# Four stacked graph networks on one core: five of 25 gathered columns picked by TensorE in the relation passes, twelve in the convolutions

## The chip, the core and the metric

The kernel runs on one core of a Trainium2 chip. Its time is the device time of one execution in microseconds (us), the median of three runs. A core has TensorE (PE, matrix products into PSUM), VectorE (DVE), ScalarE (ACT), GpSimd (POOL, here the issuer of indirect DMAs) and SyncE (SP, here the issuer of plain DMAs). Each engine works through its own instructions in order and waits on semaphores for the others.

## What is computed

Node features `x` (12,500 nodes, 16 channels) go through four graph layers, each followed by a residual sum and a layer norm. There are 400,000 edges, sorted by destination. Cut to what matters:

```python
# layer 0: a weight matrix per edge, from the edge's attributes
h = relu(edge_attr @ W1 + b1); w = (h @ W2 + b2).reshape(-1, 16, 16)
out = segment_sum(einsum('ei,eio->eo', x[src], w), dst) + x @ root
# layer 1: two graph convolutions, each over all edges
msg = (x @ W.T)[row] * norm[:, None];  out = segment_sum(msg, col) + b
# layer 2: relation matrices of 230 types, on a hyperbolic ball
msg = exp_map(einsum('ei,eio->eo', h_tan[src], rel_weight[etype]) + rel_emb[etype])
h_agg = weighted segment means of msg by dst
# layer 3: relation matrices of 90 types, times an attention term e
msg = einsum('ei,eio->eo', h[src], W_rel[rel_type]) * e;  out = segment_sum(msg, dst)
```

All five passes over the edges have one thing in common: each edge needs the row of a small node table at its source node `src`.

## The kernel before

**Passes and chunks.** Pass 0 is layer 0, passes 1 and 2 are the two graph convolutions, pass 3 and pass 4 are the relation layers with 230 and 90 types. The 400,000 edges lie as 128 partitions by 3,125 columns. A pass takes them in 125 chunks of 25 columns (`CH`), in a loop of 25 rounds by five slots (`S`).

**Table rows.** A column is 128 edges, one per partition. Its 128 table rows come in one of two ways. Either POOL issues one indirect DMA for the column (L571). Or TensorE *picks* it: the node's number is taken apart as `q * 100 + m * 25 + r`; ScalarE turns the spread code of the column into four one-hot matrices over `q`, one for each bank `m` (L849 the distance to the partition's number, L855 the one-hot); TensorE multiplies them by the table, split into two parts for accuracy (`tparts`), in 4 x 2 products of 400 columns that add up in one PSUM bank (L726); VectorE multiplies the 16 x 25 candidates by a mask of `r` (`sel`, L1282; product L1287) and adds up over the 25 (L1276). `PK` says how many of the 25 columns of a chunk are picked: before, 11 in passes 1 and 2, none elsewhere. They are handled in groups (`GRP`) of 3, 3, 3 and 2 columns that take turns in two halves of PSUM.

**A relation chunk.** ScalarE makes one-hots of the edge types (L892 distances, L901 one-hots, in two halves of 12 and 13 columns); TensorE selects each edge's matrix with them (L784, seven groups of four columns, four products a column in pass 3 and two in pass 4); VectorE multiplies by the gathered rows (L1129) and reduces (L1124), group by group, one reduction behind; between them stand small steps of the previous chunk in pass 3 (`finish`). A scan under the run mask (L804 on ScalarE, L1100 on VectorE) gives running sums per destination (L1103), which SP stores. `norms` on ScalarE (L883, L885) waits for VectorE's squared norms of the previous chunk (L1410) and stands ahead of the second half of the one-hots.

**Order.** Every engine's order is written out by hand. `chunk_in` on VectorE waits, ahead of everything else of a chunk, for its stored, gathered and loaded semaphores. SP loads a chunk's indices once the chunk five before it is done. After a pass POOL gathers the last running sum of each node (L580), VectorE does the node-wise work, and the next table is stored.

## Time and profile before

| | us |
|---|---|
| median of three runs | 17383.71 |
| lowest and highest | 17378.82, 17388.19 |
| the profiled execution | 17386.87 |
| its span | 17385.1 |

| engine | busy us | share of the span |
|---|---|---|
| PE | 10661.7 | 61% |
| DVE | 11826.2 | 68% |
| ACT | 6431.9 | 37% |
| POOL | 12857.9 | 74% |

By the first L571 of each pass and the first L580 behind it, the passes lie at 86 to 4077, 4241 to 6460, 6633 to about 8854, 9030 to 13031 and 13228 to 17226 us. Busy shares are means over these stages; what a pass is worth must be read from the chunk that repeats in it. A row of the timeline gives start, duration, engine, line, operation, tiles and count, and in brackets how long the engine had been idle and what ended it.

### The profile page before, as it was taken

What the parts mean: (1) busy time and instruction counts of PE and PEld (TensorE: products, weight loads), DVE (VectorE), ACT (ScalarE), POOL (GpSimd) and SP (SyncE); (2) the same over time, 40 slices, a digit from 0 to 9 for tenths busy, and PEclk for the clock granted to TensorE, in tenths of its full rate; (3) what the DMA queues carried; (4) which work ended last, traced back from release to release, by engine and by line L of the source; (5) the groups of instructions that cost most, each with busy time, mean ns of one, the idle gap of its engine ahead of it and who ended that gap; (6) DMA issues with size and microseconds to landing.
All of it is one profiled execution on the core that took longest, in us unless ns stands there. A gap on an engine that the chain in (4) does not pass through costs nothing.

```text
span 17385.1 us, 175951 instructions
## 1 busy us (share of the span) xinstructions
PE 10661.7 (61%) x53964; PEld 9557.6 (55%) x53964; DVE 11826.2 (68%) x12509; ACT 6431.9 (37%) x5440; POOL 12857.9 (74%) x13391
## 2 busy tenths in 40 slices
PE   6777777774999977999945555555552333333332
PEld 4555555554999977999944444544441333333332
DVE  6777777775777765777746666666664666666664
ACT  1111111112666655666634444444441222222221
POOL 6777777776777776777767777777766777777776
PEclk8888888887999998999977777777775555555555
DMA  1111111111222211222211111111111222222221
GB/s 34 27 28 28 27 28 28 27 27 27 41 41 40 40 34 33 40 41 41 39 32 38 41 41 39 40 41 41 38 40 34 46 47 45 47 47 45 46 47 30
DMA packets 811052, 649.12 MB, mean 37 GB/s; under 512 B 434919, under 2 KB 729495, under 8 KB 810245
## 3 DMA queue, kind: packets, MB, share of 16 engines
q0 software_dynamic: 428000, 138.55, 9.4%
q1 hardware_dynamic: 382882, 509.02, 9.3%
q14 instruction: 150, 1.23, 0.0%
q8 instruction: 20, 0.33, 0.0%
HBM read 480.45 MB, written 166.09 MB: 37 GB/s over the span
## 4 chain that ended last, share of the span: by engine, by line
POOL 73%; issue 24%; DVE 1%; DMA 0%; PE 0%; DVEq 0%; SPq 0%; POOLq 0%; ACT 0%; ACTq 0%
POOL deep L571 71%; POOL deep L580 3%; SPq L352 0%; DVE big L1129 0%; DVEq L926 0%; DMA wgt<-in_edge_weight 0%; PE PS L726 0%; DMA wide<-in_edge_attr 0%; DMA deep<-running,endi 0%; DVEq L1134 0%; DMA deep<-table,idx 0%; POOLq L565 0%; DVE deep L1220 0%; PE PS L748 0%; POOLq L568 0%
## 5 line engine op out<-in xcount | busy, mean ns | idle before, releaser
L571 POOL DMA_INDIRECT deep<-table,idx x12875 | 12374.5, 961 | 4205.8 <-issue 3922.1
L726 PE MATMUL PS<-tparts,hot 125*128 125x400 f32 x22000 | 4081.5, 346 | 497.2 <-DVE big L1287 324.9
L726 PEld LDWEIGHTS PS<-tparts,hot 125*128 125x128 f32 x22000 | 3997.6, 188 | 580.9 <-DVE big L1287 407.7
L1129 DVE TENSOR_TENSOR big<-PS,deep 128x768 f32<-128x768 f32 (+4 forms) x2750 | 2986.5, 1086 | 1610.6 <-DMA deep<-table,idx 957.1
L784 PE MATMUL PS<-wx,hot 115*128 115x272 f32 x12500 | 2040.5, 329 | 1939.6 <-ACT hot L901 1513.0
L784 PE MATMUL PS<-w,hot 90*128 90x256 f32 x6250 | 1517.8, 429 | 2647.5 <-DVE big L1129 2445.8
L784 PEld LDWEIGHTS PS<-wx,hot 115*128 115x128 f32 x12500 | 1933.4, 226 | 2046.6 <-issue 1539.6
L784 PEld LDWEIGHTS PS<-w,hot 90*128 90x128 f32 x6250 | 1370.8, 327 | 2794.3 <-DVE big L1129 2603.0
L687 PE MATMUL PS<-w0b_sb,big 128*128 128x256 f32 x6250 | 1909.8, 457 | 1025.5 <-DVE big L1129 989.5
L687 PEld LDWEIGHTS PS<-w0b_sb,big 128*128 128x128 f32 x6250 | 1406.1, 231 | 1594.0 <-DVE big L1129 1122.5
L855 ACT ACTIVATE hot<-deep,ones_col 128x1536 fp32r<-128x1536 bf16 x1000 | 1445.0, 1469 | 1409.1 <-PE PS L726 1369.1
L1124 DVE TENSOR_REDUCE acc<-big 128x64 f32<-128x1024 f32 (+2 forms) x1875 | 1939.8, 1035 | 18.4
L901 ACT ACTIVATE hot<-deep,ones_col 128x3072 fp32r<-128x3072 bf16 (+1 forms) x500 | 1142.0, 2284 | 1855.0 <-PE PS L784 1855.0
L1287 DVE TENSOR_TENSOR big<-PS,shared 128x1200 f32<-128x1200 f32 x1000 | 1303.6, 1304 | 603.4 <-PE PS L726 513.8
L804 ACT ACTIVATE mask<-same 128x425 bf16 x625 | 342.7, 548 | 3277.2 <-DVE msg L1103 3276.6
L849 ACT ACTIVATE deep<-wide,negbank 128x1408 bf16<-128x1408 f16 x1000 | 1387.8, 1458 | 73.6 <-DMA wide<-pick_codes 37.3
L1276 DVE TENSOR_REDUCE deep<-big 128x48 f32<-128x1200 f32 x1000 | 1291.3, 1291 | 18.3
L819 ACT ACTIVATE big<-PS,b0a_sb 128x512 f32<-128x512 f32 x1000 | 581.3, 595 | 1784.5 <-PE PS L670 1784.5
L892 ACT ACTIVATE deep<-wide,negrel 128x3200 bf16<-128x3200 bf16 x375 | 1097.3, 2957 | 58.2 <-DMA wide<-edge_types 21.9
L1124 DVE TENSOR_REDUCE msg<-big 128x64 f32<-128x1088 f32 x875 | 1011.2, 1156 | 17.3
L1473 DVE TENSOR_TENSOR sml<-term,deep 128x25 f32<-128x25 f32 x125 | 27.9, 223 | 1346.1 <-DMA deep<-table,idx 1346.1
L670 PE MATMUL PS<-atT,tabo 128*128 128x512 f32 x2000 | 883.7, 536 | 0.0
(267 smaller groups left out, 6076.6 us busy)
## 6 DMA issues: line engine op xcount, KB each, us to landing
deep<-table,idx POOLq DMA_INDIRECT x12875
wide<-edge_types SPq DMA_DIRECT2D x250, 800.0 KB, 4.3
wide<-pick_codes SPq DMA_DIRECT2D x250, 352.0 KB, 3.5
running<-msg SPq DMA_DIRECT2D x250, 212.5 KB, 2.1
running<-msg SPq DMA_DIRECT2D x250, 200.0 KB, 2.0
running<-msg SPq DMA_DIRECT2D x125, 400.0 KB, 2.5
wide<-in_edge_attr SPq DMA_DIRECT2D x125, 200.0 KB
idx<-in_src SPq DMA_DIRECT2D x625, 12.5 KB
```

The costliest lines, as they stand in the source:

```text
L571: pool.indirect_dma_start(g[:, j, 0:GW[l]], None, tab_dram[l][:, :], bass.IndirectOffsetOnAxis(ap=idx[:, s, j:j + 1], axis=0)).then_inc(ga ...
L687: last = pe.matmul(PS[:, b, (u % 2) * CC:(u % 2) * CC + CC], hsb[:, k % 2, u * P:u * P + P], w0b_sb[:, :], start=True, stop=True)
L726: last = pe.matmul(o, poneh[0:NQ, m, c], tparts[0:NQ, k, m * JC:m * JC + JC], start=m == 0 and k == 0, stop=m == BK - 1 and k == 1)
L784: last = pe.matmul(o, oneh[0:K, h, (t0 + u) * P:(t0 + u) * P + P], rhs, start=z == 0, stop=z == len(parts) - 1)
L849: last = act.activation(pdist[:, m, :], code[:, 0:NPK * P], ACT.Abs, bias=negbank[:, m:m + 1])
L855: act.activation(poneh[:, :, c], pdist[:, :, c], ACT.Relu, bias=ones_col[:, 0:1], scale=-1.0).then_inc(poneh_ready, 1)
L892: last = act.activation(dist[:, h, :], rows_b[:, HOME[s], :], ACT.Abs, bias=negrel[:, h:h + 1])
L901: act.activation(oneh[:, 0:halves, c], dist[:, 0:halves, c], ACT.Relu, bias=ones_col[:, 0:1], scale=-1.0).then_inc(oneh_ready, 1)
L1124: dve.tensor_reduce(m[:, groups[j][0], col:col + C], products(j), AXX, ALU.add)
L1129: dve.tensor_tensor(products(j), matv(l, j, n), xs, ALU.mult).then_inc(mats_free, 1)
L1276: return dve.tensor_reduce(gatv(s, l)[:, CH - n + t0:CH - n + t0 + w, :], chosen[:, i % 2, 0:w], AXX, ALU.add)
L1287: dve.tensor_tensor(chosen[:, i % 2, 0:w], PS[:, b:b + w, 0:JC].rearrange("p t (c r) -> p t c r", r=JR), sel[:, t0:t0 + w].unsqueeze(2).to ...
```

## The change

`PK` becomes 12 in passes 1 and 2, and 5 in passes 3 and 4, so POOL issues 13 and 20 indirect DMAs per chunk there in place of 14 and 25. The fourth convolution group has three columns in place of two. A relation chunk gets two groups of picks (three and two columns, of 400 columns in PSUM in pass 3, 426 in pass 4, whose table rows are 17 wide) ahead of the seven groups of matrices, on the same semaphores `mats` and `mats_free`, with PSUM banks from a table. Their one-hots (`rhot`) and distances (`rdist`) are ScalarE's, from five columns of the same codes, which one more DMA per chunk spreads. `run_mask` goes behind the one-hots. The wait for the gathers leaves `chunk_in` and stands behind the picks (`columns_in`) in all four passes. Tables of passes 3 and 4 are also split (`table_parts`), and SP waits for that ahead of their first spread; at a pass's start all five slots' loads are issued ahead of the first spread. Some buffers have new homes.

```diff
-    PK = [0, 11, 11, 0, 0]
+    PK = [0, 12, 12, 5, 5]
-    GRP = [(0, 3), (3, 3), (6, 3), (9, 2)]
+    GRP = [(0, 3), (3, 3), (6, 3), (9, 3)]
+    RGRP = [[], [], [], [(0, 3), (3, 2)], [(0, 3), (3, 2)]]
+    BANKS = [[(2 * (k % 2), 2) for k in range(8)], None, None, [(0, 3), (4, 2)] + [(4 * (i % 2), 4) for i in range(6)] + [(3, 1)],
+             [(0, 3), (3, 2), (5, 2), (0, 2), (2, 2), (4, 2), (6, 2), (3, 2), (7, 1)]]
...
             def spread_rows(l, it, s):
+                if l >= 3:
+                    c0 = (NPK - RPK) * P
+                    sp.dma_start(rcodes[:, HOME[s], :],
+                                 code_dram[bass.ds(it * S + s, 1), c0:c0 + RPK * P].rearrange("a n -> (a n)").partition_broadcast(P)
+                                 ).then_inc(rows_in[s], 16)
...
                 for s in range(S):
                     load(l, 0, s)
+                if l >= 3:
+                    sp.wait_ge(tab_st, 16 * (l + 1))
+                    sp.wait_ge(ev[f"parts{l}"], 1)
+                for s in range(S):
                     if l and s:
                         spread_rows(l, 0, s - 1)
...
+                        for i, (t0, n) in enumerate(RGRP[l]):
+                            mats_wait(l, c0 + ng * s, it, i)
+                            for u in range(n):
...
+                                for m in range(BK):
+                                    for k in range(2):
+                                        last = pe.matmul(o, rhot[0:NQ, m, c], tparts[0:NQ, k, m * pc:m * pc + pc],
+                                                         start=m == 0 and k == 0, stop=m == BK - 1 and k == 1)
+                            last.then_inc(mats, 1)
...
             def one_hots(l, it, s, first):
+                for m in range(BK):
+                    act.activation(rdist[:, m, :], rcodes[:, HOME[s], :], ACT.Abs, bias=negbank[:, m:m + 1])
                 for h in range(halves):
                     last = act.activation(dist[:, h, :], rows_b[:, HOME[s], :], ACT.Abs, bias=negrel[:, h:h + 1])
                 last.then_inc(rows_used, 1)
                 act.drain()
-                run_mask(l, it, s)
+                act.wait_ge(mats, it * (S * ng) + (o0 + ng * s - ng + NPG[l]))
+                act.activation(rhot[:, :, :], rdist[:, :, :], ACT.Relu, bias=ones_col[:, 0:1], scale=-1.0).then_inc(poneh_ready, 1)
                 for b, (t0, n) in enumerate(HALF):
...
+                run_mask(l, it, s)
                 act.drain()
...
-                dve.wait_ge(gathered[s], it * (16 * (CH - PK[l])) + (ga_base(l) + 16 * (CH - PK[l])))
                 dve.wait_ge(loaded[s], it * (16 * LOADS[l]) + (ld_base(l) + 16 * LOADS[l]))
+
+            def columns_in(l, it, s):
+
+                dve.wait_ge(gathered[s], it * (16 * (CH - PK[l])) + (ga_base(l) + 16 * (CH - PK[l])))
...
                 for j, (tiles, n) in enumerate(groups):
+                    if j == pg:
+                        columns_in(l, it, s)
```

Two places where the order moves. On VectorE in a convolution chunk, from the last picks of a chunk to the first of the next (`picks` is TensorE's signal, `gathered` POOL's), before:

```order
L1287 TENSOR_TENSOR big<-PS,shared 128x800 [waits picks]
L1276 TENSOR_REDUCE deep<-big 128x48
L1276 TENSOR_REDUCE deep<-big 128x32
L1295 TENSOR_TENSOR acc<-deep,wgt 128x25x16
L1096 REGISTER_ALU
L1100 SCALAR_TENSOR_TENSOR acc<-mask,acc 128x416 [waits masked]
L1102 COPY acc<-acc 128x16
L1103 COPY msg<-acc 128x400
L1109 REGISTER_ALU
L1282 ISA [waits loaded2,gathered2,stored0]
L1282 TENSOR_TENSOR shared<-PS,late 128x275
```

and now:

```order
L1362 TENSOR_TENSOR big<-PS,sel 128x1200 [waits picks]
L1353 TENSOR_REDUCE deep<-big 128x48 x2
L1371 TENSOR_TENSOR acc<-deep,wgt 128x25x16 [waits gathered1]
L1148 REGISTER_ALU
L1152 SCALAR_TENSOR_TENSOR acc<-mask,acc 128x416 [waits masked]
L1154 COPY acc<-acc 128x16
L1155 COPY msg<-acc 128x400
L1161 REGISTER_ALU
L1172 ISA [waits loaded2,stored0]
L1172 TENSOR_TENSOR sel<-PS,rsel 128x300
```

The gathers of the next chunk are no longer waited for ahead of its picks, and the last product has 1,200 elements in place of 800. On VectorE at a chunk's start in pass 3 (`mats` is TensorE's signal), before:

```order
L1410 TENSOR_SCALAR sml<-sml 128x25
L1129 TENSOR_TENSOR big<-PS,deep 128x1088 [waits loaded3,mats,gathered3,stored1]
L1129 TENSOR_TENSOR big<-PS,deep 128x1088 [waits mats]
L1124 TENSOR_REDUCE msg<-big 128x4x16
L1129 TENSOR_TENSOR big<-PS,deep 128x1088 [waits mats]
```

and now:

```order
L1488 TENSOR_SCALAR sml<-sml 128x25
L1172 TENSOR_TENSOR sel<-iota_f,rsel 128x125 [waits loaded4,stored4]
L1204 TENSOR_TENSOR big<-PS,sel 128x1200 [waits mats]
L1204 TENSOR_TENSOR big<-PS,sel 128x800 [waits mats]
L1193 TENSOR_REDUCE deep<-big 128x3x16
L1204 TENSOR_TENSOR big<-PS,deep 128x1088 [waits mats,gathered4]
L1193 TENSOR_REDUCE deep<-big 128x2x16
L1204 TENSOR_TENSOR big<-PS,deep 128x1088 [waits mats]
```

A mask, two products and two reductions stand ahead of the first product that needs a gathered column. On ScalarE in pass 4, before:

```order
L892 ACTIVATE deep<-wide,negrel 128x3200 [waits rows_in1]
L803 REGISTER_ALU
L804 ISA [waits chunks_done]
L804 ACTIVATE mask<-same 128x17x25
L899 REGISTER_ALU
L901 ACTIVATE hot<-deep,ones_col 128x1536 [waits mats]
L899 REGISTER_ALU
L901 ACTIVATE hot<-deep,ones_col 128x1664 [waits mats]
```

and now:

```order
L940 ACTIVATE late<-tabo,negbank 128x640 [waits rows_in1]
L940 ACTIVATE late<-tabo,negbank 128x640 x3
L942 ACTIVATE deep<-wide,negrel 128x3200
L945 REGISTER_ALU
L946 ACTIVATE rhot<-late,ones_col 128x2560 [waits mats]
L950 REGISTER_ALU
L952 ACTIVATE hot<-deep,ones_col 128x1536 [waits mats]
L950 REGISTER_ALU
L952 ACTIVATE hot<-deep,ones_col 128x1664 [waits mats]
L847 REGISTER_ALU
L848 ISA [waits chunks_done]
L848 ACTIVATE mask<-same 128x17x25
```

Five activations are new, and the mask with its wait for VectorE's finished chunks stands last.

## Rows read from the trace of the kernel before

**Rows 1.** The page's part 4, the chain that ended last, by engine.

```profile
POOL 73%; issue 24%; DVE 1%; DMA 0%; PE 0%; DVEq 0%; SPq 0%; POOLq 0%; ACT 0%; ACTq 0%
```

**Rows 2.** Instructions of L571 in passes 1, 2, 3, 4: duration ns min/median/max, first and last start.

```profile
L571 POOL DMA_INDIRECT deep<-table,idx x1750: 940/944/1197, 4240.7 to 6438.5; - x195
...
L571 POOL DMA_INDIRECT deep<-table,idx x1750: 940/944/1464, 6633.4 to 8832.2; - x195
...
L571 POOL DMA_INDIRECT deep<-table,idx x3125: 940/944/1932, 9029.7 to 12994.3; - x196
...
L571 POOL DMA_INDIRECT deep<-table,idx x3125: 940/944/1727, 13227.6 to 17199.4; - x196
```

**Rows 3.** Windows inside passes 1, 3, 4: PE, PEld, DVE, ACT, POOL, clock, DMA, GB/s.

```profile
4300.00:6400.00 2100.00, 1944.85 (x10510) 1905.22 (x10509) 1618.72 (x1551) 1404.93 (x1075) 1590.80 (x1672) 1.00 0.21 40
9200.00:12900.00 3700.00, 1901.08 (x11642) 1800.86 (x11641) 2492.85 (x3385) 1760.14 (x1051) 2811.09 (x2918) 0.75 0.18 40
13400.00:17100.00 3700.00, 1414.06 (x5824) 1277.12 (x5824) 2308.31 (x2329) 775.29 (x466) 2813.34 (x2910) 0.50 0.22 46
```

**Rows 4.** Timeline of one chunk of pass 1, TensorE and VectorE.

```profile
5000.72 16.29 PE L726 MATMUL PS<-tparts,hot 125*128 125x400 f32 x88 [1.22 <-DVE big L1287]
...
5008.30 0.99 DVE L1287 TENSOR_TENSOR big<-PS,shared 128x800 f32<-128x800 f32 x1 [0.20 <-PE PS L726]
...
5009.21 2.45 DVE L1276 TENSOR_REDUCE deep<-big 128x48 f32<-128x1200 f32 x2
...
5016.15 0.45 DVE L1282 TENSOR_TENSOR shared<-PS,late 128x275 f32<-128x275 f32 x1 [1.20 <-DMA deep<-table,idx]
...
5018.26 2.08 PE L726 MATMUL PS<-tparts,hot 125*128 125x400 f32 x10 [1.25 <-DVE big L1287]
5018.36 1.41 DVE L1287 TENSOR_TENSOR big<-PS,shared 128x1200 f32<-128x1200 f32 x1 [0.16 <-issue]
```

**Rows 5.** Timeline of VectorE in pass 3: a chunk's first products, and the next chunk's.

```profile
11001.05 1.29 DVE L1129 TENSOR_TENSOR big<-PS,deep 128x1088 f32<-128x1088 f32 x1 [7.74 <-DMA deep<-table,idx]
11002.50 1.29 DVE L1129 TENSOR_TENSOR big<-PS,deep 128x1088 f32<-128x1088 f32 x1 [0.16 <-issue]
...
11033.08 1.29 DVE L1129 TENSOR_TENSOR big<-PS,deep 128x1088 f32<-128x1088 f32 x1 [9.05 <-DMA deep<-table,idx]
```

**Rows 6.** Timeline of ScalarE, then of TensorE, in the same chunk of pass 3.

```profile
11028.34 3.06 ACT L901 ACTIVATE hot<-deep,ones_col 128x3328 fp32r<-128x3328 bf16 x1
...
11034.42 6.37 PE L784 MATMUL PS<-wx,hot 115*128 115x272 f32 x48 [2.79 <-DVE big L1129]
```

**Rows 7.** Timeline of VectorE, then of TensorE, in one chunk of pass 4.

```profile
15008.84 1.23 DVE L1129 TENSOR_TENSOR big<-PS,deep 128x1024 f32<-128x1024 f32 x1 [0.16 <-issue]
15010.23 1.22 DVE L1129 TENSOR_TENSOR big<-PS,deep 128x1024 f32<-128x1024 f32 x1 [0.17 <-issue]
...
15040.06 0.20 DVE L1473 TENSOR_TENSOR sml<-term,deep 128x25 f32<-128x25 f32 x1 [10.34 <-DMA deep<-table,idx]
...
15021.51 5.49 PE L784 MATMUL PS<-w,hot 90*128 90x256 f32 x24 [0.42 <-DVE big L1129]
```

**Rows 8.** Timeline of TensorE in pass 0: two equal groups behind idle times of different length.

```profile
3036.24 2.93 PE L687 MATMUL PS<-w0b_sb,big 128*128 128x256 f32 x6 [4.14 <-DVE big L1129]
...
3067.60 1.56 PE L687 MATMUL PS<-w0b_sb,big 128*128 128x256 f32 x6 [2.71 <-DVE big L1129]
```

**Rows 9.** Timeline at pass ends (POOL) and in the node-wise work between them (VectorE).

```profile
6460.20 0.94 POOL L580 DMA_INDIRECT deep<-running,endi  x1 [20.74 <-DMA running<-msg]
...
9041.51 0.42 DVE L1046 TENSOR_TENSOR w<-big,w 90x256 fp32r<-90x256 f32 x1
...
13031.09 0.94 POOL L580 DMA_INDIRECT deep<-running,endi  x1 [35.83 <-DMA running<-msg]
...
13216.00 1.82 DVE L1467 TENSOR_REDUCE na<-Y 125x100 f32<-125x1600 f32 x1
...
17226.24 1.31 POOL L580 DMA_INDIRECT deep<-running,endi  x1 [25.91 <-DMA running<-msg]
```

More of the change, by code:

```diff
@@ L85, in build_gnn @@
     JC = C * JR
-    GRP = [(0, 3), (3, 3), (6, 3), (9, 2)]
+    PW = [0, C, C, C, C + 1]
+    PCOL = [(w * JR + 1) // 2 * 2 for w in PW]
+    GRP = [(0, 3), (3, 3), (6, 3), (9, 3)]
+    RGRP = [[], [], [], [(0, 3), (3, 2)], [(0, 3), (3, 2)]]
+    NPG = [len(g) for g in RGRP]
     NGR = len(GRP)
@@ L90, in build_gnn @@
     PRIOR = [3, 3, 2, 2, 5]
-    PICKED = [1, 2]
+    PICKED = [1, 2, 3, 4]
+    RPK = PK[3]
+    assert PK[4] == RPK and 3 * (C + 1) * JR <= 1600
     LOADS = [3, 2, 2, 1, 2]
     NAT = (CH + 7) // 8
-    GROUPS = [[(slice(k, CH, 8), len(range(k, CH, 8))) for k in range(8)], None, None] + 2 * [[(slice(t, t + n), n) for t, n in QUADS]]
+    GROUPS = [[(slice(k, CH, 8), len(range(k, CH, 8))) for k in range(8)], None, None] + [
+        [(slice(CH - PK[l] + t, CH - PK[l] + t + n), n) for t, n in RGRP[l]] + [(slice(t, t + n), n) for t, n in QUADS] for l in (3, 4)]
+    BANKS = [[(2 * (k % 2), 2) for k in range(8)], None, None, [(0, 3), (4, 2)] + [(4 * (i % 2), 4) for i in range(6)] + [(3, 1)],
+             [(0, 3), (3, 2), (5, 2), (0, 2), (2, 2), (4, 2), (6, 2), (3, 2), (7, 1)]]
     MATS = [0, 3, 4]
@@ L239, in build_gnn @@
         flat_b = Y[:, :].bitcast(BF16)[:, 0:TILES]
-        VT = shared[:, 0:13 * NQ].rearrange("p (b n) -> p b n", n=NQ)
+        ohr = Y[:, :].bitcast(BF16)[:, 0:CH * NJ].rearrange("p (t r) -> p t r", r=NJ)
+        VT0, VT = (t[:, 0:13 * NQ].rearrange("p (b n) -> p b n", n=NQ) for t in (big2, late))
         tabo = sb("tabo", [P, NJ * 17])
-        rsel = late[:, 0:NCH * NPK]
-        sel = shared[:, 0:NPK * JR].rearrange("p (t r) -> p t r", r=JR)
+        rsel = sb("rsel", [P, NCH * NPK], BF16)
+        sel = sb("sel", [P, NPK, JR])
+        rhot = sb("rhot", [P, BK, RPK * P], F32R)
+        rdist = Z.bitcast(BF16)[:, 0:RPK * BK * P].rearrange("p (m n) -> p m n", m=BK)
+        rcodes = tabo[:, 0:3 * RPK * P // 2].bitcast(F16).rearrange("p (k n) -> p k n", k=3)
         chosen = big2[:, 0:6 * JC].rearrange("p (g t c r) -> p g t c r", g=2, t=3, r=JR)
+        rprod = big2[:, 0:3200].rearrange("p (k n) -> p k n", k=2)
         w0blk = tabo[:, 0:8 * HID].rearrange("p (k h) -> p k h", h=HID)
@@ L592, in transposes, with node_product @@
                 last.then_inc(ready, 1)
-            def node_product(kron, done):
+            def node_product(kron, done, of=VT):
                 for b, (c0, n) in enumerate(BLK):
-                    last = pe.matmul(PSF[0:NQ, c0:c0 + n], VT[0:n, b, :], kron[0:n, 0:n], start=True, stop=True)
+                    last = pe.matmul(PSF[0:NQ, c0:c0 + n], of[0:n, b, :], kron[0:n, 0:n], start=True, stop=True)
                 last.then_inc(done, 1)
@@ L646, in mats_wait @@
             def mats_wait(l, m, it, j):
-                slots, n = SLOTS[l], len(GROUPS[l])
-                back = j - slots + 1 if j >= slots else max(k for k in range(n) if k % slots == j % slots) + 1 - n
-                pe.wait_ge(mats_free, it * (S * n) + (m + NPR + back))
+                n, (b, w) = len(BANKS[l]), BANKS[l][j]
+                ago = next(d for d in range(1, n + 1) if BANKS[l][j - d][0] < b + w and b < sum(BANKS[l][j - d]))
+                pe.wait_ge(mats_free, it * (S * n) + (m + MFREE + j - ago + 1))
             NG0 = len(GROUPS[0])
@@ L831, in flip @@
                     for b in range(0, len(blocks), 4):
-                        c0, n = blocks[b][0], min(4, len(blocks) - b) * P
-                        last = act.copy(to[:, c0:c0 + n], PS[:, 4 + b // 4, 0:n])
+                        c0, n = blocks[b][0], sum(k == P for _, k in blocks[b:b + 4]) * P
+                        if n:
+                            last = act.copy(to[:, c0:c0 + n], PS[:, 4 + b // 4, 0:n])
+                    b, (c0, n) = len(blocks) - 1, blocks[-1]
+                    if n < P:
+                        last = act.copy(to[0:n, c0:c0 + P], PS[0:n, 4 + b // 4, b % 4 * P:b % 4 * P + P])
                     last.then_inc(flip_sb, 1)
@@ L1131, in matrices @@
                         reduce(j - 1)
-                    if amid is not None:
-                        amid(j)
+                    if amid is not None and j >= pg:
+                        amid(j - pg)
                     dve.drain()
@@ L1156, in pick_codes @@
                 then(dve.scalar_tensor_tensor(codes, h, float(P), g, ALU.mult, ALU.add))
[L1157 removed]
+                dve.scalar_tensor_tensor(rsel[:, :].rearrange("p (k t) -> p k t", t=NPK), h, -float(JR), f, ALU.mult, ALU.add)
                 dve.drain()
@@ L1472, in _, with whole_term @@
                     chunk_in(4, it, s)
-                    then(dve.tensor_tensor(sml[:, 1, :], term[:, s, :], gatv(s, 4)[:, :, C], ALU.add))
-                    matrices(4, it, s, C)
+                    nodes_of_bank(4, it, s, iota_f[:, 0:JR])
+                    def whole_term(i):
+                        if i == 1:
+                            dve.tensor_tensor(sml[:, 1, :], term[:, s, :], gatv(s, 4)[:, :, C], ALU.add)
+                    matrices(4, it, s, C, whole_term)
                     then(dve.tensor_tensor(m[:, :, 0:C], m[:, :, C:2 * C], bc_c(sml[:, 1, :]), ALU.mult))
```

99 lines of the change are left out of this document (63 added, 36 removed).

## The prediction

> **What bounds the kernel now.** First the chain of waits: three quarters of it is POOL and most of the rest is the issue time between POOL's instructions [rows 1]. Then the gathers by pass: 1,750 in 2,197.8 us and 3,125 in 3,964.6 and 3,971.8 us, that is 1.256, 1.269 and 1.271 us for one without a break [rows 2]. So a chunk takes 14 x 1.256 = 17.6 us in passes 1 and 2 and 25 x 1.27 = 31.7 and 31.8 us in passes 3 and 4. POOL sets the pace in every pass. Last the chunks, for what comes next once POOL is faster. In pass 1 VectorE waits only 1.20 us for the gathers, and TensorE works 16.29 us of the 17.54 between two chunks: both have little room [rows 4]. In pass 3 VectorE waits 9.05 us, in pass 4 10.34 us [rows 5, 7].
>
> **Gathers removed.** If POOL stayed the bound, 1 x 1.256 x 125 = 157 us would go in each of passes 1 and 2 and 5 x 1.27 x 125 = 794 us in each of passes 3 and 4, 1,902 us in all. POOL's new chunk is 16.3 us and 25.4 us. Each pass has to be asked whether another engine is slower than that.
>
> **Passes 1 and 2.** TensorE gets 96 products a chunk for 88, at 16.29 / 88 = 0.185 us: 17.8 us, already over the 17.6 of now. It also has to wait for PSUM. Its third group of a chunk needs the half that VectorE's first product of that chunk frees, and that product stands behind VectorE's end of the chunk before. Now it is 9.96 us from the start of the last product of a chunk (5008.30) to TensorE's resumption (5018.26) [rows 4]. The wait for the gathers in it (1.20) goes, except for a gap of about 0.15 as between other instructions: 8.9 us. The last product grows from 800 to 1,200 elements, 0.99 to 1.41 us, and I give its reduction the same 0.4: 9.7 us. Behind it TensorE has groups three and four, 48 x 0.185 = 8.9 us. The chunk becomes 18.6 us, 1.0 more than now: the moved wait and the one gather less give nothing, since TensorE and VectorE now chase each other. 125 x 1.0 and about 3 us for the later first spread make +129 us a pass, **+258 us** for both. Bounds: TensorE alone (17.8 us a chunk, +57 us in both), and half a microsecond more hand-over (+380).
> The Trainium skill, page "TensorE: Matmul & The Clock Gate", section "Back-to-back issue gap", gives N/2.4 + 2.5 ns between products at full clock, 169 ns for 400 columns. Here the clock is fully granted [rows 3] and the step is 185 ns [rows 4]; by the page (an estimate) the chunk would be 17.8 us and the whole sum about 200 us lower. The trace measures the same instruction, so it decides.
>
> **Pass 3.** VectorE's own work is 11033.08 - 9.05 - 11001.05 = 23.0 us a chunk [rows 5]. Added are products of 1,200 and 800 elements (1.41 + 0.99), their reductions (2.45 for such a pair) [rows 4], the mask of 125 elements (between 0.2 for 25 and 0.45 for 275 [rows 4, 7], with its gap 0.5) and about 0.1 of drains: 5.45. VectorE needs 28.4 us; POOL's 25.4 lies under it, and the moved gather wait finds its columns long there. TensorE has 40 x 0.185 + 100 x 6.37/48 = 20.7 us at the full clock [rows 4, 6]. It runs ahead of VectorE with the picks of the next chunk (their banks are free from VectorE's fifth matrix group on), but then waits for VectorE's first product of the new chunk, about 5 us. In pass 0 an idle time of 4.14 us is followed by six products in 2.93 us, one of 2.71 us by the same six in 1.56 [rows 8]: behind the longer one the engine is at its lower clock of 1.2 GHz. So the first matrix group, 16 products, runs at that level: a product of 256 columns takes 5.49/24 = 0.229 us with the granted clock at 0.50 [rows 3, 7], one of 272 columns 0.243 us, the group 3.9 us. It starts when the first product ends, 2.1 us into the chunk, and is there at 6.1; VectorE wants it at 4.6. That is 1.6 us a chunk. The next groups catch up. The chunk is 30.0 us (bounds: 28.4, and 31.5 when the lower clock reaches the second group too).
> ScalarE gets some 4 x 0.7 + 2.4 us more, by 3.06 us for 3,328 elements [rows 6], and has some 21 of 30 us to do; the second half of its one-hots ends 6.3 us behind VectorE's squared norms (3 us of table loads and norms, then the 3.06) and is wanted at about 11 us. So its work is hidden, and so is the mask, now last, which is read a chunk later; were this cover gone, 3 us a chunk is at stake. The extra DMA lies under 14 us of slack.
> The start costs: splitting the table, 4.7 us behind 9041.9 [rows 9], then by estimate the spread (6), distances and one-hots (11), the first 24 picks, partly at the lower clock (7): VectorE starts at 9070.8. The end of the pass is 9070.8 + 125 x 30.0 + 8 = 12,829 against 13,031 [rows 9]: **-202 us**.
>
> **Pass 4.** VectorE's own work is 15040.06 - 10.34 - 15008.84 = 20.9 us [rows 7]. Added: picks of 1,275 and 850 elements (1.49 + 1.04 at 1.04 ns an element, from 1.41 - 0.99 for 400 [rows 4]), reductions 2.5, mask 0.5, gaps 0.3: 5.8. The chunk is 26.7 us, again over POOL's 25.4. TensorE stood at 0.50 of its clock throughout [rows 3]. Even there 40 x 0.38 + 50 x 0.229 = 26.6 us is no more than VectorE; the picks would come 1.6 us late at worst (28.6 us a chunk), and only if twice the work left the clock there; at 16.3 us busy of 17.5 it is fully granted in pass 1 [rows 3, 4]. ScalarE has 13 us to do. Start: the split ends 4.9 us behind 13217.8, the first product follows by the same steps at 13247.4; end 13247.4 + 125 x 26.7 + 3.3 = 16,588 against 17,226 [rows 9]: **-638 us** (bounds -790 with POOL as the pace, -400 with TensorE late).
>
> **Sum.** 258 - 202 - 638 = -582, and +3 for four small extra steps between passes: -579. The profiled execution took 17,386.9 us, 3.2 over the median, so 16,808 there and 16,805 as a median.
>
> **Rivals.**
> *Pass 3 without the clock's loss.* If the 5 us of idle leave the clock up, the pass is 200 us shorter: 16,600. For it: mean clock 0.75 there [rows 3] is with idle times of 12 us. Against: rows 8. 13%.
> *Heavier hand-overs.* Each wait newly met late costs 0.5 to 1 us in all four passes: 17,050. For it: three engines now alternate with little room. 14%.
> *POOL still paces.* If VectorE's added work overlapped its waits in full, the time would be 17,387 - 1,902 = 15,485. Against it: 23.0 + 5.45 > 25.4. 3%.
> *Slower than before.* The mechanism is TensorE at 1.2 GHz through pass 3. Its 40 picks then take 40 x 0.357 (0.229 x 400/256) and its 100 matrix products 24.3 us, 38.6 us a chunk against 31.7: +860 in that pass, and 17,387 + 258 + 860 - 638 = 17,870. It decides from 34.8 us a chunk, where the losses equal pass 4's gain, with about four fifths of the products at the lower clock. For it: pass 4 sat at 0.50 throughout. Against: that was with TensorE busy 38% of the time [rows 3]; now it is busy in long runs. 6%.
> *No net effect*, the parts cancelling within 0.2%: 2%.
>
> **Numbers.** The forecast has 62%, with a range of its own of 16,650 to 17,000. The range for 8 in 10 takes in the first rival and most of the second: 16,550 to 17,150. Within 0.2% is about what a measurement of this kernel can't tell from no change. Faster 0.91, same 0.02, slower 0.07.
>
> **What would show it.** Right: in passes 1 and 2 TensorE idles about 0.8 us a chunk behind VectorE's product while POOL waits for SP's loads; chunks of 18.6, 30.0 and 26.7 us; no wait for gathers on VectorE; in pass 3 VectorE waits for TensorE at its first matrix group. Wrong: gathers still awaited, or a chunk of pass 3 under 29 or over 31.5 us, or VectorE waiting for picks in pass 4.

## The result, and the profile after

| | us |
|---|---|
| before, median beside the changed kernel | 17385.95 |
| after, median of four runs | 17165.39 |
| lowest and highest | 17160.04, 17167.06 |
| the ratio, with its 95% interval | 0.9872 (0.9857 to 0.9888) |
| forecast, and its range | 16805 (16550 to 17150) |

The kernel is 1.3% faster where 3.3% was forecast, and the time lies just above the range. By pass, from the first gather to the first gather of the pass's end (L571 and L580 before, L601 and L610 after), with the mean time between two chunks' ends on VectorE in brackets:

| pass | before | forecast | after |
|---|---|---|---|
| 0 | 3991.8 (31.7) | no change | 3978.8 (31.6) |
| 1 | 2219.5 (17.6) | 2349 (18.6) | 2419.9 (19.18) |
| 2 | 2220.5 (17.6) | 2350 (18.6) | 2417.0 (19.17) |
| 3 | 4001.4 (31.5) | 3799 (30.0) | 3960.5 (31.17) |
| 4 | 3998.6 (31.8) | 3361 (26.7) | 3434.1 (27.27) |

The measured changes, -13, +200, +197, -41 and -565, make -222 us; 360 us are missing from the forecast, 71, 67, 161 and 73 of them in passes 1 to 4. Each of the four was forecast too short. Pass 0, which the change leaves alone, came out 13 us shorter.

The page of the profile of after: busy time by engine, the row of the granted clock, the two rows of instruction packets (DMA packets that bring code), and part 4 by engine, which answers to [rows 1].

```profile
PE 12881.2 (75%) x65965; PEld 11693.0 (68%) x65965; DVE 13324.3 (78%) x13771; ACT 7962.4 (46%) x6691; POOL 11383.4 (66%) x11891
...
PEclk8888888887999997999997888888888666666666
...
q14 instruction: 152, 1.25, 0.0%
q8 instruction: 24, 0.39, 0.0%
...
DVE 29%; POOL 20%; DVEq 20%; PE 19%; issue 11%; DMA 1%; SPq 0%; ACT 0%; POOLq 0%; ACTq 0%
```

POOL had 73% of the chain; now VectorE with its sequencer (DVEq) has 49%, and POOL's 20% is mainly pass 0. The granted clock is 0.88 in pass 3 and 0.69 in pass 4. Windows inside passes 3 and 4 (the columns of [rows 3]):

```profile
9500.00:13200.00 3700.00, 2739.70 (x16528) 2623.26 (x16528) 3101.33 (x4015) 2395.60 (x1652) 2256.39 (x2372) 0.88 0.19 44
13700.00:17000.00 3300.00, 2428.30 (x10855) 2225.99 (x10853) 3026.99 (x3026) 1431.91 (x1075) 2324.25 (x2398) 0.69 0.26 58
```

**Passes 1 and 2.** TensorE, then VectorE, in pass 1; these answer to [rows 4].

```profile
5517.24 17.73 PE L756 MATMUL PS<-tparts,hot 125*128 125x400 f32 x96 [1.31 <-DVE big L1362]
5536.40 17.74 PE L756 MATMUL PS<-tparts,hot 125*128 125x400 f32 x96 [1.43 <-DVE big L1362]
...
5507.25 1.41 DVE L1362 TENSOR_TENSOR big<-PS,sel 128x1200 f32<-128x1200 f32 x1 [1.63 <-PE PS L756]
5508.58 2.87 DVE L1353 TENSOR_REDUCE deep<-big 128x48 f32<-128x1200 f32 x2
5511.60 0.94 DVE L1371 TENSOR_TENSOR acc<-deep,wgt 128x400 f32<-128x400 f32 x1 [0.16 <-issue]
...
5515.78 1.41 DVE L1362 TENSOR_TENSOR big<-PS,sel 128x1200 f32<-128x1200 f32 x1 [0.19 <-issue]
```

Once a chunk TensorE stands for 1.31 to 1.43 us until VectorE has taken the first product of the next chunk. From the last product's start (5507.25) to TensorE's resumption (5517.24) it is 9.99 us, forecast as 9.7.

**Pass 3.** VectorE at a chunk that begins with its loop's jump back (answers to [rows 5]), and TensorE in the same and the next chunk:

```profile
11007.69 0.18 DVE L1488 TENSOR_SCALAR sml<-sml 128x25 f32<-128x25 f32 x1
11012.07 0.29 DVE L1172 TENSOR_TENSOR sel<-iota_f,rsel 128x125 f32<-128x125 f32 x1 [4.20 <-issue]
...
11018.06 1.29 DVE L1204 TENSOR_TENSOR big<-PS,deep 128x1088 f32<-128x1088 f32 x1 [1.62 <-PE PS L828]
...
11020.69 1.29 DVE L1204 TENSOR_TENSOR big<-PS,deep 128x1088 f32<-128x1088 f32 x1 [0.44 <-PE PS L828]
...
11014.03 12.91 PE L828 MATMUL PS<-wx,hot 115*128 115x272 f32 x80 [9.52 <-DVE big L1204]
...
11044.92 12.84 PE L828 MATMUL PS<-wx,hot 115*128 115x272 f32 x80 [6.11 <-DVE big L1204]
```

From the list of waits in 9500 to 13200 us (total us, times, longest), VectorE's two longest:

```profile
DVE big L1204 <- PE PS L828: 240.4, 225, 1.8
DVE sel L1172 <- issue: 114.2, 71, 5.3
```

Two losses stand here. VectorE waits 2.06 us (1.62 and 0.44) for its first two matrix groups, behind 6 to 9 us in which TensorE did nothing. By the starts of the single products in the trace, the first 21 of the 80 behind the 9.52 us follow each other at 0.227 us and the rest at 0.126: the lower clock level, then the upper. And at each of the loop's 23 jumps back VectorE stands at L1172 with nothing that the profile shows to wait for, 4.20 us here and 4.6 on average. The chunks of four slots take 30.5 to 30.8 us, the 23 with a jump 34.6. (The last interval of the pass is 9.3 us, since no next chunk's work stands in it; a mean over all 25 of the fifth slot, 33.4, hides that.)

**Pass 4.** VectorE, two chunks' starts (answers to [rows 7]):

```profile
15502.09 0.29 DVE L1172 TENSOR_TENSOR sel<-iota_f,rsel 128x125 f32<-128x125 f32 x1 [0.89 <-issue]
...
15506.91 1.22 DVE L1204 TENSOR_TENSOR big<-PS,deep 128x1024 f32<-128x1024 f32 x1 [0.24 <-issue]
...
15529.31 0.29 DVE L1172 TENSOR_TENSOR sel<-iota_f,rsel 128x125 f32<-128x125 f32 x1 [0.32 <-issue]
```

27.2 us without one wait for another engine over 0.5 us: VectorE is the pace.

### The profile page after: what moved, and what is told of

It reads as the page before. It is cut to its first block, busy times and chain, and to the rows that moved or that the text cites. A ratio compares the mean times of both kernels' runs of the same rounds, so it can differ in the third digit from the quotient of the medians.

```text
span 17163.0 us, 204283 instructions
## 1 busy us (share of the span) xinstructions
PE 12881.2 (75%) x65965; PEld 11693.0 (68%) x65965; DVE 13324.3 (78%) x13771; ACT 7962.4 (46%) x6691; POOL 11383.4 (66%) x11891
## 3 DMA queue, kind: packets, MB, share of 16 engines
q14 instruction: 152, 1.25, 0.0%
## 4 chain that ended last, share of the span: by engine, by line
DVE 29%; POOL 20%; DVEq 20%; PE 19%; issue 11%; DMA 1%; SPq 0%; ACT 0%; POOLq 0%; ACTq 0%
POOL deep L601 17%; PE PS L756 13%; DVE big L1204 12%; DVEq L1209 8%; PE PS L828 5%; DVEq L978 5%; DVE big L1362 4%; DVEq L1156 3%; DVE acc L1152 3%; POOL deep L610 3%; DVE deep L1353 2%; DVEq L1367 2%; DVEq L1153 2%; DVE acc L1371 1%; DVE sel L1172 1%
## 5 line engine op out<-in xcount | busy, mean ns | idle before, releaser
L601 POOL DMA_INDIRECT deep<-table,idx x11375 | 10899.3, 958 | 5286.2 <-issue 3430.7
L756 PE MATMUL PS<-tparts,hot 125*128 125x400 f32 x24000 | 4443.8, 345 | 530.2 <-DVE big L1362 351.8
L756 PEld LDWEIGHTS PS<-tparts,hot 125*128 125x128 f32 x24000 | 4358.7, 188 | 615.1 <-DVE big L1362 434.5
L814 PE MATMUL PS<-tparts,rhot 125*128 125x400 f32 (+1 forms) x10000 | 2169.1, 381 | 236.2 <-ACT rhot L946 236.2
L903 ACT ACTIVATE hot<-deep,ones_col 128x1536 fp32r<-128x1536 bf16 x1000 | 1552.7, 1576 | 1583.3 <-PE PS L756 1543.5
L814 PEld LDWEIGHTS PS<-tparts,rhot 125*128 125x128 f32 x10000 | 2062.5, 211 | 292.9 <-issue 236.5
L1362 DVE TENSOR_TENSOR big<-PS,sel 128x1200 f32<-128x1200 f32 x1000 | 1408.2, 1408 | 1012.6 <-PE PS L756 924.0
L828 PE MATMUL PS<-w,hot 90*128 90x256 f32 x6250 | 1325.3, 377 | 889.6 <-DVE big L1204 889.5
L828 PEld LDWEIGHTS PS<-w,hot 90*128 90x128 f32 x6250 | 1160.0, 272 | 1042.7 <-DVE big L1204 1040.8
L897 ACT ACTIVATE deep<-wide,negbank 128x1536 bf16<-128x1536 f16 x1000 | 1494.5, 1565 | 79.0 <-DMA wide<-pick_codes 42.7
```

Of the source, the lines that this page charges most:

```text
L601: pool.indirect_dma_start(g[:, j, 0:GW[l]], None, tab_dram[l][:, :], bass.IndirectOffsetOnAxis(ap=idx[:, s, j:j + 1], axis=0)).then_inc(ga ...
L756: last = pe.matmul(o, poneh[0:NQ, m, c], tparts[0:NQ, k, m * JC:m * JC + JC], start=m == 0 and k == 0, stop=m == BK - 1 and k == 1)
L814: last = pe.matmul(o, rhot[0:NQ, m, c], tparts[0:NQ, k, m * pc:m * pc + pc], start=m == 0 and k == 0, stop=m == BK - 1 and k == 1)
L828: last = pe.matmul(o, oneh[0:K, h, (t0 + u) * P:(t0 + u) * P + P], rhs, start=z == 0, stop=z == len(parts) - 1)
L897: last = act.activation(pdist[:, m, :], code[:, 0:NPK * P], ACT.Abs, bias=negbank[:, m:m + 1])
L903: act.activation(poneh[:, :, c], pdist[:, :, c], ACT.Relu, bias=ones_col[:, 0:1], scale=-1.0).then_inc(poneh_ready, 1)
```

## The experiments

All kernels are the changed one with the edit shown. "Chunk" is the mean time between two chunks' ends. e1, e5, e7, e9, e11 and e16 to e18 were run four times, the others once; in e1 and e9 the four runs lie within 14 us. Passes and chunks are read from one profiled execution each.

**e1, eleven columns in the convolutions.**

```diff
-    PK = [0, 12, 12, 5, 5]
-    GRP = [(0, 3), (3, 3), (6, 3), (9, 3)]
+    PK = [0, 11, 11, 5, 5]
+    GRP = [(0, 3), (3, 3), (6, 3), (9, 2)]
```

> The changed kernel with eleven picked columns in passes 1 and 2 as before, all else as changed (five in the relation passes, the gather wait behind the picks, loads ahead of the first spread). Theory: what costs passes 1 and 2 is TensorE and VectorE alternating at twelve columns. With eleven, TensorE needs 16.3 us a chunk, the hand-over plus two groups 8.9 + 7.4 = 16.3 us, and POOL's 14 x 1.256 = 17.6 us is the pace again: each pass, first gather to first L610, goes from 2,418 to about 2,225 us, the whole from 17,165 to about 16,775. Rival: the moved wait, the later first spread or the new homes of buffers cost it: the passes stay near 2,400 us and the time at 17,100 to 17,165.

16832.5 us, ratio 0.968 (0.9664 to 0.9696). Passes 1 and 2 take 2255.2 and 2250.8 us, passes 3 and 4 stay (3961.4, 3431.6). So the twelfth column alone costs 165 us a pass, and the changed kernel without it is 3.2% faster than before. The passes were expected at 2,225 us and the whole at 16,775; they are 30 and 26 us over that, and 36 and 30 us over the kernel before, with the same number of columns. VectorE still waits for gathers, now in the middle of a chunk and ahead of the steps that free TensorE's banks (4500 to 6300 us):

```profile
DVE acc L1371 <- DMA deep<-table,idx: 84.4, 64, 1.6
```

That the moved wait is what costs the 30 us is a guess; no run moves it back.

**e2, TensorE kept busy in pass 3.** 24 products that nothing reads stand behind the picks of each chunk.

```diff
+                        if l == 3:
+                            for u in range(24):
+                                pe.matmul(PS[:, 6, 0:pc], wx[0:K, 0, 0, 0:P], tparts[0:K, 0, 0:pc], start=True, stop=True)
```

> The changed kernel with 24 products of 400 columns that nobody reads, behind the picks of each chunk in pass 3, where TensorE would idle; the result is not touched. Theory: VectorE's wait for the first matrix groups (2.0 us a chunk) is there because TensorE's clock has fallen in the idle time of 6 to 9 us. With the idle time filled, 16 products take 2.1 instead of 3.6 us, the wait goes to about zero, a chunk of pass 3 goes from 31.2 to 29.2 us, the pass from 3,960 to about 3,720, the whole to about 16,925. Rival: the wait is the hand-over itself (the first matrix group cannot start before VectorE's first product ends), whatever the clock: the chunk stays at 31.2 us or grows.

16977.5 us; pass 3 takes 3774.7 us in place of 3960.5, its chunk 29.6 us in place of 31.2; passes 1 and 4 stay. TensorE behind its picks; then the window of pass 3; then VectorE's waits in it:

```profile
11000.03 4.64 PE L819 MATMUL PS<-tparts,wx 115*128 115x400 f32 x24
11006.04 8.52 PE L831 MATMUL PS<-wx,hot 115*128 115x272 f32 x64 [1.37 <-DVE big L1207]
```

```profile
9500.00:13200.00 3700.00, 3225.22 (x20210) 3083.56 (x20209) 3257.71 (x4214) 2492.07 (x1727) 2338.43 (x2442) 0.97 0.20 47
```

```profile
DVE sel L1175 <- issue: 104.1, 74, 4.8
...
DVE big L1207 <- PE PS L831: 37.5, 41, 3.4
```

Behind an idle time of 1.37 us 64 products of 272 columns take 8.52 us, 0.133 us each, and none of them is at the lower level; in after, behind 9.52 us, the first 80 took 12.91 us, 2.3 more than 80 x 0.133. More work on TensorE made VectorE's waits for it fall from 240 to 38 us in this window and the granted clock rise from 0.88 to 0.97. The wait at the jump (L1175) stays: 3.1 to 4.8 us, 3.9 on average, and the 23 chunks with it take 32.8 us where the others take 28.7 to 29.9.

The filling has a price. It makes TensorE's loop longer, and now TensorE's code is loaded in the loop as well: q8 has 241 packets for 24, and once a round TensorE stands some 3.1 us ahead of its picks (the profile puts most of it down to VectorE):

```profile
q8 instruction: 241, 3.95, 0.1%
...
PE PS L814 <- DVE big L1207: 64.6, 21, 3.3
```

**e3, other groups in the convolutions:** 4, 4, 2, 2 columns for 3, 3, 3, 3, so that less stands on VectorE between a chunk's last product and the next chunk's first. (The buffer of the products grows by a third, and a counting row that the mask `sel` is made from is read from SBUF, not from a copy in PSUM, so one copy on VectorE goes; making `sel` takes 0.47 us either way.)

```diff
-    GRP = [(0, 3), (3, 3), (6, 3), (9, 3)]
+    GRP = [(0, 4), (4, 4), (8, 2), (10, 2)]
```

> The changed kernel with the twelve picks of passes 1 and 2 in groups of 4, 4, 2, 2 columns instead of 3, 3, 3, 3 (the comparison's counting row is read from SBUF, since the fourth bank is now used). Theory: the loop that sets the 19.2 us is hand-over (10.1 us from the last product of a chunk to TensorE's resumption) plus the last two groups. Two first groups of 4 cover 64 x 0.185 = 11.8 us of it and the last two take 5.9 us, so TensorE never waits: a chunk is TensorE's own 17.8 to 18.1 us, a pass about 2,280 us, the whole about 16,890. Rival: the chunk is set by VectorE's or ScalarE's own work or by the jump back of the loop: it stays above 18.8 us.

16804.3 us; passes 1 and 2 take 2203.9 and 2202.3 us, a chunk 17.44, a little less than before the change and with one gather less. A window of pass 1:

```profile
4500.00:6300.00 1800.00, 1800.00 (x9910) 1799.80 (x9910) 1490.45 (x1342) 1315.47 (x930) 1283.40 (x1349) 1.00 0.20 42
```

TensorE has no idle time left, and 1800 / 9910 = 0.182 us is the step of a product of 400 columns; 96 of them are the whole chunk. So the loss in passes 1 and 2 was the hand-over between the two engines, and not a lack of either. Pass 3, whose own code the edit doesn't touch (the copy that goes stands ahead of it), became 73 us longer, some 60 of them in the 23 chunks with a jump: 37.2 us for 34.6, with 5.8 to 6.6 us at L1172; the others take 30.6 to 30.9.

**e4, the run mask back ahead of the one-hots of the picks.**

```diff
                 act.drain()
+                run_mask(l, it, s)
                 act.wait_ge(mats, it * (S * ng) + (o0 + ng * s - ng + NPG[l]))
...
-                run_mask(l, it, s)
                 act.drain()
```

> The changed kernel with the run mask back ahead of the one-hots in passes 3 and 4 (behind the distances). Theory: the mask waits for the chunk two before to be done, which in pass 3 is near the end of the chunk before; ScalarE would stand there some 10 us with the picks' one-hots behind it, TensorE's picks come 5 us or more late, and pass 3 grows by 5 to 10 us a chunk, 600 to 1,200 us; pass 4, where a chunk is done without delay, stays within 1 us a chunk. Rival: the place of the mask is of no weight, since VectorE is the bound: both passes as changed, 17,165.

17927.0 us, slower than before. Pass 3 has a chunk of 37.3 us (+6.1), pass 4 stays at 27.25. The waits of the three engines in the same window of pass 3:

```profile
ACT mask L848 <- DVE msg L1155: 1674.0, 99, 17.5
...
PE PS L814 <- ACT rhot L947: 1148.1, 99, 11.9
...
DVE big L1204 <- PE PS L814: 833.5, 198, 7.8
```

The mask waits up to 17.5 us for VectorE's end of the chunk before; the one-hots, the picks and VectorE follow it one after the other, and the 40 picks take 10.24 us, behind 11.57 us in which TensorE did nothing, for 7.43. The place of the mask in the change is worth more than the whole change brings.

**e5 to e8, in other conditions.** Here the kernel before takes 24,625 us, and the engines wait long for loads of indices and attributes in every pass. Ratios to before can still be taken, but the pace is another.

e5 is e2 and e3 together. e6 is e5 with VectorE's loop of pass 3 over two rounds:

```diff
-            with dve.Fori(1, IT) as it:
-                for s in range(S):
-                    hyper_chunk(it, s, lambda j, s=s: finish(it - (s == 0), (s - 1) % S, j))
+            with dve.Fori(0, (IT - 1) // 2) as two:
+                for it in (two * 2 + 1, two * 2 + 2):
+                    for s in range(S):
+                        hyper_chunk(it, s, lambda j, s=s, it=it: finish(it - (s == 0), (s - 1) % S, j))
```

e7 is e5 with four columns picked in passes 3 and 4 (`RGRP` becomes groups of three and one):

```diff
-    PK = [0, 12, 12, 5, 5]
+    PK = [0, 12, 12, 4, 4]
```

e8 is the changed kernel with a longer body of VectorE's loop of pass 4 (a drain computes nothing):

```diff
+                    if s == 2:
+                        for _ in range(60):
+                            dve.drain()
```

> Groups of 4, 4, 2, 2 in passes 1 and 2 and the filled idle time in pass 3 together. Theory: the two effects lie in different passes and add up: -361 us (17,165 to 16,804) and -188 us (17,165 to 16,977), so 16,617 us. Rival: pass 3 of the kernel with 4, 4, 2, 2 was 73 us longer than that of the changed kernel, by one chunk in five; if this stays, 16,615 to 16,690.

> The kernel of e5 with VectorE's loop in pass 3 written out for two rounds (ten chunks) instead of one. Theory: one chunk in five is 3 to 5 us longer since VectorE's jump back to the loop's start has to fetch code (343 instructions a round; instruction packets are in the trace in pass 3 alone); with half the jumps, one chunk in ten is, and pass 3 loses 12 x 3 to 5 = 36 to 60 us. Rival: the longer chunk is a wait for a store or a load that falls on slot 0 of every round: it stays one in five and the pass stays as in e5.

> The kernel of e5 with four picked columns in passes 3 and 4 instead of five. Theory: VectorE is the bound of both, a column's product and reduction cost it 0.85 us, and POOL's 21 x 1.27 = 26.7 us is near: a chunk of pass 3 goes from 29.6 to 28.8 us, one of pass 4 from 27.3 to 26.8 us (POOL again), together -160 us against e5, about 16,455. Rival: five is right where it is; VectorE's waits for TensorE or the gathers take back what its work loses: same as e5 within 30 us.

> The changed kernel with 60 empty instructions (drains) in one slot (slot 2) of VectorE's loop of pass 4, 271 instructions a round before and 331 now. Theory: a loop of that length no longer stays on the engine (246 and 271 a round show no instruction packets, 285 and 343 do); instruction packets appear in pass 4, some 5 a round, and the chunk with the jump back grows from 27.8 to 30 us or more, beside about 3 us for the drains themselves in slot 2. Rival: the long chunk in pass 3 has to do with that pass's waits: no packets, 27.8 us stays.

e5 gave 22943.5 us (0.9295), e6 22929.8, e7 23223.7 (0.9411), e8 23183.3. By time none of the four questions is answered, since POOL waits for its indices in nearly every chunk of pass 3; a row of e7's waits there, in 13500 to 18000 us:

```profile
POOL deep L601 <- DMA idx<-in_src: 2102.9, 93, 26.8
```

Some 22 us of waiting and 21 gathers of 1.25 us make up its 48 us a chunk. With four columns pass 3 is 205 us longer than with five (6109 and 5904 us): there the gathers are the pace again.

**e9 to e12, the same four kernels in conditions like the first** (before: 17385.7 us).

> The kernel of e5 again: in e5 to e8 loads and gathers landed much later than in all runs before, the kernel of before included (24,625 us), so their passes say nothing of engine times. Theory and numbers as for e5: 16,617 us, or up to 16,690 if pass 3 keeps the longer chunk.

e9: 16563.7 us, ratio 0.9527 (0.9511 to 0.9543). Passes 1 and 2 2202 us each, pass 3 3788.5, pass 4 3432.6. By pass, the gains of e2 (186) and e3 (216 + 215), less the 14 us by which pass 3 is longer than in e2, give 17165 - 603 = 16562. The expectation, 16,617, took e3's gain as a whole, with the 73 us that its pass 3 lost. Those did not come back: the chunks with a jump take 33.5 us here and took 37.2 in e3, though VectorE runs the same code at the same place.

> The kernel of e6 again. Theory: half the jumps back, pass 3 loses 36 to 60 us against e9, and one chunk in ten is long. Rival: one in five stays long.

e10: 16515.4 us. Pass 3 takes 3747.9 us, 41 less, with half of the jumps; behind the first chunk of the pass q14 brings 86 packets for 122. But one chunk in ten was expected to be long, and one in five is: 32.4 us behind a jump of VectorE's, 32.3 where VectorE runs on without one, 28.8 to 29.1 the others. Its own wait, L1175, is gone there; it waits for TensorE instead, whose loop still jumps once a round (9500 to 12700 us):

```profile
PE PS L814 <- DVE big L1207: 59.0, 19, 3.4
...
DVE sel L1175 <- issue: 51.6, 64, 4.4
DVE big L1207 <- PE PS L831: 40.1, 20, 4.1
```

So with the filling, of the 4.6 us by which a chunk at a round's end is longer in e9 (33.5 us), VectorE's jump is only the last 1.2.

> The kernel of e7 again. Theory: 28.8 us a chunk in pass 3 and 26.8 in pass 4, about 16,455 us. Rival: within 30 us of e9. Where loads landed late (e7) it was the slower one, since every gather more counts there.

e11: 16608.7 us, 0.9551 (0.9535 to 0.9567). Pass 4 takes 3368.2 us, 64 less, as expected: POOL's 21 gathers and VectorE are about level, a chunk is 26.7 us. Pass 3 was expected to gain and takes 132 us more, with 37.2 us in the chunks with a jump. TensorE and VectorE at one:

```profile
11021.21 4.64 PE L819 MATMUL PS<-tparts,wx 115*128 115x400 f32 x24
11034.77 13.34 PE L831 MATMUL PS<-wx,hot 115*128 115x272 f32 x80 [8.92 <-DVE big L1207]
...
11032.83 0.26 DVE L1175 TENSOR_TENSOR sel<-iota_f,rsel 128x100 f32<-128x100 f32 x1 [6.16 <-issue]
```

The longer the jump stalls VectorE, here 5.7 to 7.5 us, the longer TensorE idles; then its clock is lower when it goes on (some 26 of the 80 products at 0.227 us). The filling that was enough in e9 (clock 0.98 in 9500 to 12700 us) is not here (0.92). Why the stall is longer than in e9 isn't known.

> The kernel of e8 again. Theory: instruction packets in pass 4 and a chunk with the jump back of 30 us or more. Rival: none, 27.8 us stays.

e12: 17225.0 us. The drains cost 2.4 us in their own slot; the chunk with the jump is 27.76 us, as without them, and no instruction packets come in the loop, though it now has 331 instructions. In the kernel before, VectorE's loop of pass 3 has 286 by the trace and gets them. The theory that a loop's length alone decides fell; the place in the code remained.

**e13 to e18: place against length.** e13 is e5 with four columns in pass 4 alone. e14 and e15 move VectorE's loop of pass 3 in the code by 43 and 86 drains ahead of it; e16 is e13 with the loop of e6. All six ran in conditions like those of e5 (before: 25,082 us for e13 to e16, 24,724 for e17 and e18).

```diff
+            for _ in range(86):
+                dve.drain()
             with dve.Fori(1, IT) as it:
```

> The changed kernel with groups of columns (0 to 3), (4 to 7), (8, 9), (10, 11) in passes 1 and 2 and 24 further products a chunk in pass 3 (their results are not used), and with five columns picked by TensorE in pass 3 but four in pass 4. Theory: the parts are separate, since each acts in its own pass. Passes 1 and 2 as in e9 (2,202 us each), pass 3 as in e9 (3,788 us, up to 60 either way by where VectorE's loop lies in the code), pass 4 as in e11 (3,368 us). So about 16,564 - 64 = 16,500 us, 16,440 to 16,560. Rival: pass 4 at four columns was quick only because all of the relation arrays were one column smaller: pass 4 stays at 3,430 us and the kernel at 16,560.

> As e13_five_and_four, with 43 drain instructions on VectorE once, ahead of its loop of pass 3, so that this loop begins 43 instructions further on in the code. Theory: the long wait at the loop's jump back in pass 3 is code that has to be loaded again, and where the loop starts in the code sets how many blocks it spans. Then the chunk with the jump changes by 2 us or more against e13 (pass 3 by 40 to 90 us) in this run or in e15, and the number of instruction packets with it. Rival: the wait depends on the loop's length alone; then pass 3 is as in e13 within 10 us in both.

> As e14_shift43, with 86 drain instructions ahead of the loop. Theory: at one of the three starts (e13, e14, e15) the loop spans a block fewer, the instruction packets of pass 3 become fewer or none, and the chunk with the jump is shorter by 2 us or more. Rival: all three alike within 0.5 us a jump.

> As e13_five_and_four, with VectorE's loop of pass 3 over two rounds, so that it jumps back half as often. Theory: as e10 against e9, 41 us less in pass 3: about 16,450 us, 16,400 to 16,500, 0.947 of the kernel before. Rival: the gain of e10 came from the place of its loop in the code, not from the fewer jumps; then it is within 20 us of e13.

> The kernel of e15_shift86 again. Its trace showed 7 instruction packets in pass 3 where e13 and e14 have 121, but on that chip loads of indices were the pace of pass 3 and hid what a jump costs. Theory: with no code to load at the jump, the chunk with the jump is under 1 us longer than the others in pass 3 (2.8 us in e9, whose loop of pass 3 has the same code at the same place as e13's), so that pass 3 takes 3,788 - 25 x 2.1 = about 3,735 us (3,715 to 3,750), pass 4 3,368 us, and the whole 16,564 - 53 - 64 = about 16,447 us. Rival: the packets run ahead of the jump and cost nothing; the chunk stays 2.8 us longer and the whole at 16,500 us.

> The kernel of e13_five_and_four again, as the control of e17: 121 packets in pass 3, its chunk with the jump 2.8 us longer than the others, pass 3 3,788 us, pass 4 3,368 us, 16,500 us in all. Rival: as e17 within 15 us.

Medians: e13 23430.3, e14 23474.0, e15 23398.0, e16 23415.3, ratio 0.9337 (0.9294 to 0.9381). By time these can't be told apart. The traces can: behind the first chunk of pass 3 e13 and e14 have 122 packets on q14, e15 has 7. e17 (the kernel of e15) and e18 (that of e13) repeat the pair: 22965.9 us, 0.9288 (0.9265 to 0.9310), and 23042.0 us, 0.9320 (0.9298 to 0.9342). The intervals overlap, so for the whole kernel the gain stays unsure. Pass 3 is 5888.5 us against 5925.0, but pass 0, where the two don't differ, is 38 us shorter in e17 as well. VectorE's wait at L1176 in 13500 to 18000 us, e18 first, then e17:

```profile
DVE sel L1176 <- issue: 95.9, 57, 6.5
```

```profile
DVE sel L1176 <- issue: 22.5, 57, 0.6
```

The rows of instruction packets in the page of the profile (all of the kernel: packets, MB, share), e18 first, then e17:

```profile
q8 instruction: 241, 3.95, 0.1%
q14 instruction: 152, 1.25, 0.0%
```

```profile
q8 instruction: 241, 3.95, 0.1%
q14 instruction: 38, 0.31, 0.0%
```

The edit touches VectorE's code alone and q14 alone follows; q8 followed TensorE's in e2 and stays. The same loop, 86 instructions further on, jumps back without packets on q14 and with at most 0.6 us; at e18's 23 jumps it is 3.2 to 6.5. (One wait of 4.45 us stays, where the pass first comes to the loop.) The chunks with a jump take 49.5 us for 51.5, the others 45.2 to 46.1 in both. What it would give in conditions like the first was not measured.

## Why the prediction was wrong

Two steps failed. In pass 3 the forecast put VectorE's jump back at nothing, and it costs 4.0 us at each of 23 jumps, 91 us. And the chains were summed too short: 0.6 us a chunk in passes 1, 2 and 4, and as much in the ordinary chunks of pass 3. That POOL would stop being the pace, and what would take its place in each pass, was right: no gather is awaited in passes 1 to 4.

**Passes 1 and 2: mechanism right, size off.** The forecast named the chase of TensorE and VectorE, which e3 shows. The term was 1.0 us a chunk and measured 1.6. The hand-over was put at 9.7 us and took 9.99, mainly by small gaps on VectorE between the product, `sel` and the copies. It counted nothing between TensorE's end of group four and VectorE's start on it (0.33 us: the last product begins 9.05 us behind group three's first, where 48 x 0.182 is 8.7). And the chunk at the loop's jump is 0.8 us longer, 0.16 for each; the forecast had read one ordinary chunk. The step of 0.185 us was a little high, since 16.29 / 88 takes in the last product's end; e3's row says 0.182. The rule of the Trainium skill that the prediction set aside (page "TensorE: Matmul & The Clock Gate", section "Back-to-back issue gap"), 169 ns by its formula, doesn't agree with the trace: at 169 ns the 9910 products would take 1675 us, and they filled 1800. The section itself gives the formula for an isolated product.

**Pass 3: two terms.** The clock's loss was named and real (e2), and counted as 1.6 us where VectorE waits 2.06: the first group's wait, 1.62, was right, but the lower clock reached into the second group (0.44), which the upper bound of the chunk had allowed for. With some smaller gaps beside it the ordinary chunk is 30.6 us for 30.0, 77 us in 125 chunks. The second term was missing: the stall at the jump, 23 x (34.6 - 30.6) = 91 us. In the kernel before, it lay under the wait for the gathers, 7.74 and 9.05 us [rows 5]: the trace has 121 packets on q14 there too, but the chunks with a jump take 31.0 us, less than the mean. The prediction said of other covers what they hide, not of this one. The pass's start and end were right, 42 us where 49 were counted; 77 + 91 - 7 is the 161.

**Pass 4: right but for small gaps.** VectorE is the pace and never waits for picks. The added work was put at 5.8 us and is 6.3: 4.82 us from `sel` to the first matrix product (15502.09 to 15506.91), the second reduction with its gap, 1.15, and 0.32 ahead of `sel`. The jump adds 0.13. So 26.7 became 27.27. TensorE was not late with its picks, so the clock, 0.69 for 0.50, cost nothing here.

**Cover.** "3 us a chunk is at stake" for the mask was half of it: e4 lost 6.1, since not only ScalarE's own work but the picks behind it come late, at a lower clock.

**Rivals.** *Heavier hand-overs* came nearest in time and describes three of four passes (+0.6 us a chunk), but by several small things rather than by one. *Pass 3 without the clock's loss* is refuted by e2: the loss is there, and taking it away gives 186 us. *POOL still paces* failed in all four. *Slower than before*: the clock was 0.88 in pass 3, not 0.50. *No net effect*: the interval of the ratio, 0.9857 to 0.9888, excludes it. The range ended at 17,150 because it took the passes' bounds as if they would offset each other: together (+380 for +258, 31.5 us a chunk, -400) they reach 17,350. All four missed the same way, and 0.6 us of each chunk by the same habit: durations were added up with few of the gaps between them, and read from one chunk, not from a round.

**What comes of it.** The best that was measured is e10, 16515 us, 0.950 of before in a single run; e9 has 0.9527 with an interval. By estimate, four columns in pass 4 (-64, e11 against e9) and a loop placed as in e17 would give about 16,470: of the jump only 23 x (33.5 - 32.3) = 28 us can be had while TensorE's loop jumps as in e10. In the other conditions that kernel has the lowest ratio of all, though its interval overlaps with e5's.

## What to carry to other kernels

When two engines chase each other through a shared buffer, cost the change by the chain between a chunk's last release and the next chunk's first, with every gap in it; then cut that chain (smaller last groups, e3) before giving either engine more. When a wait that was long in every chunk goes, ask what lay under it that no row names: the loop's jump, an engine's clock. Read at least one whole round of the loop, not one chunk. When work is added to a loop, even idle work, look whether its code is now loaded at each jump (e2).
